# Unread products in the gaps of TensorE, later turns, panels awaited in parts, and a bias add moved behind a barrier

## The chip, the cores and the metric

The kernel runs on 1 core of one Trainium2 chip. The metric is the device time of one execution in microseconds (us). TensorE (PE) multiplies, VectorE (DVE) and ScalarE (ACT) work on tiles, GpSimd (POOL) fills, SyncE (SP) issues the transfers. TensorE's clock has two levels here, 2.4 GHz (shown as 1.00) and 1.2 GHz (shown as 0.50).

## The reference, cut to what matters

Four graph layers over 3125 nodes with 64 channels and 53125 edges sorted by dst, each followed by a residual sum and a layer norm:

```
x = layernorm(x + gcn2(x))              # h = x @ W; segment_sum(h[src], dst), twice, relu between
e = silu(silu([x[src], x[dst], d] @ eW1 + eb1) @ eW2 + eb2)
x = layernorm(x + silu([x, segment_sum(e, src)] @ nW1 + nb1) @ nW2 + nb2)
x = layernorm(x + relu(h_x + h_mu + relu(segment_sum(cat, src) @ W4.T)))     # message layer
x = layernorm(x + sum_k L^k x @ W[k] / k! + bias)    # polynomial of the graph Laplacian, k = 0..10
```

## The kernel before, in words

The nodes are cut into 25 blocks of 125 (B). The graph stands in SBUF as `t.mat`, a matrix of edge counts in bf16, 25 panels of 125 x 3128. A sum over edges for one block of nodes is 25 products of a 125x128 piece of `t.mat` with a 125x192 piece of `parts` (a float32 table split in three bf16 parts). Each layer is a block of its own, with a barrier of all engines behind it.

The layers in order of time: placing the edges and counting (to about 335 us), two GCN layers (`gcn_layers`, 335 to 459), the edge network (`edge_network`: a preparation block, 459 to 476, and a main block, 476 to 909), the message layer (`message_layer`, 909 to 1004), and the polynomial layer (`polynomial_layer`, 1004 to 1561).

`gcn_layers`: DVE reduces each sum (L1037), adds x, takes statistics (L1008, L1010), and scales finished rows chunk by chunk (`scale_rows`, L1021 to L1026); a chunk is scaled one sum after its last statistics.

`edge_network`, preparation: PE turns the node table (L1144) and multiplies it with eWb (L1154); ACT and DVE split the product in three parts (L1169, L1172, L1190, L1193). DVE adds the node bias nb2 to `t.xb` (L1180) ahead of that split. The edge rows of block 0 are being loaded meanwhile (`load_rows`, L1107 to L1110; `srow` and `drow`).

Main block: SP first loads rows of block 1 and panel 0 of `t.mat` back from DRAM. On DVE `rows_to_hot(0, 0)` (L1429, L1433) turns `srow` into one-hots, `dst_rows_to_hot(0, 0)` (L1437) does so with `drow`, and `split_p(0, 0)` (L1405 to L1411) splits the product that PE made in `product_p(0, 0)` (L1246) of the tile `xs[0]`, staged by ACT at L1334. Then come 25 blocks of 5 groups: `layer1` (L1258, L1264), silu, `layer2` (L1274), bias, silu, split, and `by_src` (L1287), the sum by source. After the last block the drain works off what is left: `layer2`, three `by_src`, `node1` (L1296, L1297), `node2` (L1302), while DVE centres the rows (L1511) and adds the last output (L1420), and ACT loads the table for the square root (L1392).

Panels 16 to 24 of `t.mat` hold temporaries of the edge network (`room`). SP loads panels 16 to 18 in the drain (L1240) and 19 to 24 in the message layer (L1579), two transfers each, all on the semaphore `tail_in`.

`message_layer`: PE turns the rows (L1692), multiplies them (L1708, L1726) in 7 groups; DVE splits the results into `parts` (L784 to L790). Then PE waits for all of `tail_in` and for all of `parts_ready`, and runs 25 sums (`spread`, L777) into two alternating banks. DVE takes each (L1851 to L1858), with statistics, and `centre` for each finished chunk, which waits for ACT's square root (`take_root`, L1637). ACT then scales (`set_x3`, L1645, L1649), PE turns the chunk (`turn_x3`, L1741), ACT keeps it (`keep_x3`, L1656), PE multiplies (`top_product`, L1753) and ACT keeps that (L1663). The chunks are blocks 0-3, 4-7, 8-11, 12-15, 16-19, 20-22, 23-24. `turn_x3(i)` stands behind sum 4i+7, `top_product(i)` behind the sum after it. ACT's order for each chunk is `take_root(i)`, `set_x3(i)`, `keep_y(i-1)`, `mask_y(i-1)`, `keep_x3(i)`. On DVE `centre(5)` stands ahead of the last reduction:

```
if b == NB - 1:
    take_stats(b - 1)
    centre(len(chunks) - 2)
dve.wait_ge(sums, b + 1)
```

`polynomial_layer`: 50 products (L1970), then 10 terms of 25 sums each (L1984). The first term waits for `last_kept`, a copy on DVE (L2028) that stands behind its bias add (L2014).

Of the kernel before, what the change touches and what calls it, by code (L numbers as in the profile page):

```python
# [12 lines left out]
P = 128  # L13
# [21 lines left out]
HEAD = 16  # L35
SPAN = 112
# [803 lines left out]
def gcn_layers(nc, a, c, t, l0, l1):  # L840

    with ExitStack() as s:
# [18 lines left out]
        chunks = [slice(lo, hi) for lo, hi in ((0, 8), (8, 16), (16, 23), (23, NB))]  # L861
# [187 lines left out]
def edge_network(nc, a, c, t, rows_d, m2_d, w, l2):  # L1049
# [14 lines left out]
    with ExitStack() as s:  # L1064
# [6 lines left out]
        o = NB * 3 * H  # L1071
        x1T = room[:, o:o + 2 * (NB + 1) * B].bitcast(F32)
        o += 2 * (NB + 1) * B
        srow = [room[:, o + i * DENSE:o + (i + 1) * DENSE] for i in range(2)]
# [4 lines left out]
        o += 2 * DENSE  # L1079
# [34 lines left out]
        tile_groups = [range(g, min(g + 4, NB)) for g in range(0, NB, 4)]  # L1114
        q_part = lambda g, r: q[0:B, tile_groups[g][0]:tile_groups[g][-1] + 1, r, :]
# [3 lines left out]
        with nc.Block() as block:  # L1119
# [19 lines left out]
            def _(pe):  # L1139
# [9 lines left out]
                for g, blocks in enumerate(tile_groups):  # L1149
                    pe.wait_ge(x1t_ready, g + 1)  # L1150
                    if g >= 2:
                        pe.wait_ge(q_cut, g - 1)
                    for i, b in enumerate(blocks):
                        last = nc.tensor.matmul(ps_z2[g % 2][0:B, i * H:(i + 1) * H], x1T[:, b * B:(b + 1) * B],  # L1154
                                                eWb[:], start=True, stop=True)
                    last.then_inc(q_ps, 1)

            @block.scalar
            def _(act):
                for g, blocks in enumerate(tile_groups):  # L1160
# [4 lines left out]
                                   ).then_inc(x1t_ready, 1)  # L1165
                for g in range(len(tile_groups) + 1):
# [8 lines left out]
            def _(dve):  # L1175
# [3 lines left out]
                dve.wait_ge(turned, len(tile_groups))  # L1179
                S(nc.vector.tensor_tensor(t.xb[:], t.xb[:], nb2[:].unsqueeze(1).broadcast_to([B, NB, D]), ALU.add))  # L1180
# [18 lines left out]
        (panels_in, rows_hot, staged, pre_done, e1_ready, z2_done, biased, silu2_done,  # L1199
         cut, mid_done, split_done, hot_ready, seg_done, agg_ready, n1_ready, z1_ready, out_ready, out_kept, stats, aggregated, xs_ready, p_ps, p_ready,  # L1200
         step) = map(sem, (
             "panels_in", "rows_hot", "codes_staged", "pre_done", "e1_ready", "z2_done", "biased", "silu2_done",
             "high_cut", "mid_done", "split_done", "onehots_ready", "seg_done", "agg_ready", "n1_ready", "z1_ready", "out_ready", "out_kept", "stats_taken", "aggregated",
             "xs_ready", "p_product", "p_ready", "net_step"))
# [9 lines left out]
        with nc.Block() as block:  # L1214
            @block.sync
            def _(sp):
# [21 lines left out]
                for i in range(HEAD, HEAD + 3):  # L1238
                    for to, of in spans(t.mat[:, i, :], m2_d[i]):
                        sp.dma_start(to, of).then_inc(l2.tail_in, 16)  # L1240

            @block.tensor
            def _(pe):
# [77 lines left out]
                product_p(0, 0)  # L1321
# [3 lines left out]
                by_src(z, 0, NG - 3)  # L1325
                by_src(z, 0, NG - 2)
                by_src(z, 0, NG - 1)
                node1(z, 0)
                node2(z, 0)

            @block.scalar
            def _(act):
# [51 lines left out]
                stage_x(0, 0)  # L1384
# [10 lines left out]
            def _(dve):  # L1395
# [29 lines left out]
                def rows_to_hot(b, k):  # L1425

                    if not first(b):
# [3 lines left out]
                        .broadcast_to([P, ST, DUP])).then_inc(staged, 1)  # L1431
                    dve.wait_ge(src_in[k], 8 * (b - k) + 16)
# [62 lines left out]
                rows_to_hot(0, 0)  # L1495
                dst_rows_to_hot(0, 0)
                split_p(0, 0)
# [21 lines left out]
def l2_weights(nc, ctx):  # L1519
# [6 lines left out]
    w.w_in, w.tail_in = (ctx.enter_context(nc.semaphore(n)) for n in ("L2_weights_in", "L2_tail_in"))  # L1526
# [11 lines left out]
def message_layer(nc, a, c, t, m2_d, l2):  # L1538


    with ExitStack() as s:
# [20 lines left out]
         kept, var, root, centred, x3_set, x3_scaled, x3_turned, x3t, w_top_in, w_top_set, x3_last, y_ps, y_kept, y_masked, deg_set, droot, deg_step, step) = map(sem, (  # L1562
# [3 lines left out]
             "x3_last_scaled", "y_product", "y_kept", "y_masked", "deg_set", "deg_root", "degrees_done", "msg_step"))  # L1566
# [5 lines left out]
        with nc.Block() as block:  # L1572
            @block.sync
            def _(sp):
                sp.wait_ge(feat_clear, 1)
                sp.dma_start(feat[D:D + 2, :], a["node_vec1"].partition_broadcast(2)).then_inc(nv_in, 16)
                for i in range(HEAD + 3, NB):
                    for to, of in spans(t.mat[:, i, :], m2_d[i]):
                        sp.dma_start(to, of).then_inc(l2.tail_in, 16)  # L1579
# [12 lines left out]
            def _(act):  # L1592
# [32 lines left out]
                act.wait_ge(deg_step, 1)  # L1625
# [60 lines left out]
            def _(pe):  # L1686
# [42 lines left out]
                pe.wait_ge(l2.tail_in, 32 * (NB - HEAD))  # L1729
                pe.wait_ge(parts_ready, len(groups))  # L1730

                def turn_x3(i):
# [3 lines left out]
                    else:  # L1736
                        pe.wait_ge(x3_last, 1)
# [31 lines left out]

            @block.vector  # L1770
            def _(dve):
# [47 lines left out]
                v.reciprocal(t.scale[:], t.root_deg[:]).then_inc(deg_step, 1)  # L1819
# [23 lines left out]
                for b in range(NB):  # L1843
# [17 lines left out]
                    if b >= 2 and b - 2 in ends[:-2]:  # L1861
# [11 lines left out]
                                ALU.mult).then_inc(x3_last, 1)  # L1873
# [738 lines left out]
```

## Time and profile before

| | |
|---|---|
| time, median of 3 runs | 1563.66 us (1562.77 to 1566.78) |
| time of the profiled execution | 1562.83 us |
| its span, first to last instruction | 1560.8 us |
| mean granted clock | 0.972 |
| PE busy | 1392.3 us, 89% of the span |
| DVE busy | 1207.8 us, 77% |
| ACT busy | 623.9 us, 40% |

Busy time is the sum of an engine's instructions. The granted clock is a mean, so a stretch at 0.75 is half its time at each level. In a row of the timeline, what stands in brackets is the idle time of the engine before the instruction and what ended it. PE rows are matmuls, PEld rows their weight loads, SPq rows the issue of transfers.

### The profile page before, as it was taken

The numbers are of one execution on the slowest core, as the hardware profiler recorded it, in microseconds if no ns is written. First come the engines' busy times: TensorE is split into PE (matmuls) and PEld (weight loads), VectorE is DVE, ScalarE is ACT, GpSimd is POOL, SyncE is SP. The second block draws the span as 40 slices with busy tenths as digits, with TensorE's granted clock in tenths as the row PEclk, the third lists the DMA queues.
The fourth block names the chain that finished last, engine by engine and source line by source line (L and its number), as shares of the span: only waits on it lengthen the run. The fifth ranks groups of instructions, "written<-read, shape, count | busy, mean of one in ns | idle before, by whom it ended". The sixth has DMA issues, their size and how long they took to land. (4 is left out here: it accounts for less than half of the span.)

```text
span 1560.8 us, 43036 instructions
## 1 busy us (share of the span) xinstructions
PE 1392.3 (89%) x16795; PEld 1286.9 (82%) x16795; DVE 1207.8 (77%) x3558; ACT 623.9 (40%) x1167; POOL 40.3 (3%) x81
## 2 busy tenths in 40 slices
PE   1845488889988999999999979899999999999997
PEld 1534466679986888888888849899999999999997
DVE  6899888855557888888888876677677677677676
ACT  0279799941116777777777742400000000000000
POOL 2111000000000000000000000000000000000000
PEclk9989799989999999999999979999999999999999
DMA  1000045430015454453232170000000000000000
GB/s 28 2 0 0 6 142 160 145 108 23 2 42 140 131 153 129 121 157 112 78 115 77 39 183 1 6 2 2 1 2 2 1 2 2 2 2 2 2 7 18
DMA packets 36900, 83.82 MB, mean 54 GB/s; under 512 B 22829, under 2 KB 23861, under 8 KB 36767
## 3 DMA queue, kind: packets, MB, share of 16 engines
q1 hardware_dynamic: 33633, 81.46, 18.4%
q8 instruction: 93, 1.52, 0.4%
q10 hardware_dynamic: 2880, 0.37, 0.2%
q14 instruction: 38, 0.31, 0.1%
q0 software_dynamic: 256, 0.15, 0.1%
HBM read 60.76 MB, written 21.14 MB: 52 GB/s over the span
## 5 line engine op out<-in xcount | busy, mean ns | idle before, releaser
L1984 PE MATMUL L_psA<-L_parts,mat 125*128 125x192 bf16 x3125 | 258.6, 246 | 0.4 <-issue 0.4
L1984 PE MATMUL L_psA<-second,mat 125*128 125x192 bf16 x3125 | 259.0, 246 | 0.0
L1984 PEld LDWEIGHTS L_psA<-L_parts,mat 125*128 125x128 bf16 x3125 | 257.9, 98 | 0.6 <-issue 0.6
L1984 PEld LDWEIGHTS L_psA<-second,mat 125*128 125x128 bf16 x3125 | 257.6, 98 | 0.6
L1264 PEld LDWEIGHTS L_ps_pre<-L_drow,mat 128*128 128x128 bf16 x2250 | 128.3, 98 | 30.0 <-issue 0.6
L1931 ACT COPY L_wk<-L_Wk 128x64 f32<-128x64 f32 x8 | 1.6, 242 | 378.1 <-PE L_psA L1984 378.1
L2040 DVE TENSOR_REDUCE L_sumr<-L_psA 125x64 f32<-125x192 f32 x225 | 80.4, 357 | 71.7 <-PE L_psA L1984 71.6
L1264 PE MATMUL L_ps_pre<-L_drow,mat 128*128 128x32 bf16 (+3 forms) x2250 | 132.7, 212 | 0.0
L684 PE MATMUL ps_count<-onehot 128*128 128x125 bf16 x1200 | 107.4, 219 | 15.2 <-DVE onehot L647 7.7
L1453 DVE TENSOR_TENSOR L_e<-L_e,mat 128x512 f32<-128x512 f32 x125 | 86.1, 689 | 40.4 <-ACT L_e L1351 40.4
L647 DVE TENSOR_TENSOR onehot<-iota_bf,codes 128x1024 bf16<-128x1024 bf16 x150 | 100.6, 686 | 18.0 <-PE ps_count L684 16.8
L886 PE MATMUL L_psA<-L_gparts,mat 125*128 125x192 bf16 x1250 | 111.2, 249 | 0.2 <-DVE L_sumr L993 0.2
L886 PEld LDWEIGHTS L_psA<-L_gparts,mat 125*128 125x128 bf16 x1250 | 106.6, 101 | 1.0 <-DVE L_sumr L993 0.4
L1287 PE MATMUL L_ps_agg<-L_hot,mat 128*128 128x125 bf16 x1500 | 103.5, 219 | 3.8 <-DVE mat L1458 3.8
L684 PEld LDWEIGHTS ps_count<-onehot 128*128 128x128 bf16 x1200 | 87.4, 98 | 23.2 <-DVE onehot L647 12.5
L1258 PE MATMUL L_ps_pre<-mat,L_pp 125*128 125x512 bf16 x375 | 102.4, 381 | 2.8 <-DVE L_pp L1411 2.8
L1445 DVE TENSOR_TENSOR L_e<-L_ps_z,L_eb 128x512 f32<-128x512 f32 x125 | 85.8, 686 | 21.4 <-PE L_ps_z L1274 19.8
L1287 PEld LDWEIGHTS L_ps_agg<-L_hot,mat 128*128 128x128 bf16 x1500 | 93.8, 98 | 5.6 <-DVE mat L1458 4.2
L1350 ACT ACTIVATE mat<-L_e 128x512 bf16<-128x512 f32 x125 | 78.9, 631 | 39.1 <-DVE L_e L1445 36.0
L1355 ACT CAST mat<-L_e 128x512 bf16<-128x512 f32 x125 | 77.0, 616 | 38.3 <-DVE L_e L1453 37.4
L1458 DVE TENSOR_TENSOR mat<-L_e,mat 128x512 bf16<-128x512 f32 x125 | 85.0, 680 | 0.3 <-ACT mat L1355 0.3
L426 PE MATMUL ps_slot<-rows,ohr 128*128 128x208 bf16 x450 | 45.9, 258 | 43.2 <-DVE rows L409 38.7
(329 smaller groups left out, 2387.3 us busy)
## 6 DMA issues: line engine op xcount, KB each, us to landing
L_drow<-rows_d SPq DMA_DIRECT2D x25, 728.0 KB
mat<-m_d SPq DMA_DIRECT2D x25, 684.2 KB
mat<-rows_d SPq DMA_DIRECT2D x25, 640.0 KB, 4.4
m_d<-panel SPq DMA_DIRECT2D x13, 684.2 KB
m_d<-xb SPq DMA_DIRECT2D x12, 684.2 KB
L_drow<-rows_d SPq DMA_DIRECT2D x25, 84.5 KB
mat<-m_d SPq DMA_DIRECT2D x25, 79.4 KB
m_d<-panel SPq DMA_DIRECT2D x13, 79.4 KB
```

What stands on the lines that cost most here:

```text
L647: nc.vector.tensor_tensor(to.rearrange("p e (m t) -> p e m t", t=DUP), c.iota1_bf[:].rearrange("p (m t) -> p m t", t=DUP).unsqueeze(1).bro ...
L684: last = nc.tensor.matmul(to, rows, cols[:, 0:B], start=True, stop=more is None)
L886: last = nc.tensor.matmul(acc(layer, b)[:, 0:3 * D], t.mat[0:B, kb, b * B:b * B + P], parts[layer][:, kb].rearrange("p r d -> p (r d)"), s ...
L1258: nc.tensor.matmul(ps_pre[bank][:, 0:hi - lo], pp[k][:, r, :], srow[k][0:B, lo:hi], start=(r == 0), stop=False)
L1264: last = nc.tensor.matmul(ps_pre[bank][:, to:to + n], w, drow[k][:, of:of + n], start=False, stop=(r == 2 and cc == pieces[-1][0]))
L1287: last = nc.tensor.matmul(ps_agg[k][:, 0:B], e2_parts[bank][:, part, i * H:(i + 1) * H], hot[bank][:, i, 0:B], start=(cc == 0 and part == ...
L1350: nc.scalar.activation(e2_parts[buf(k, g)][:, 0, :], e, ACT.Silu)
L1445: nc.vector.tensor_tensor(e2[buf(k, g)][:].rearrange("p (i h) -> p i h", h=H), ps_z2[bank][:].rearrange("p (i h) -> p i h", h=H), eb2[:].u ...
L1453: nc.vector.tensor_tensor(e, e, e2_parts[buf(k, g)][:, 0, :], ALU.subtract).then_inc(cut, 1)
L1458: nc.vector.tensor_tensor(part[:, 2, :], e2[buf(k, g)][:], part[:, 1, :], ALU.subtract).then_inc(split_done, 1)
L1984: last = nc.tensor.matmul(ps[:, 0:3 * D], t.mat[0:B, kb, b * B:b * B + P], parts[src][:, kb].rearrange("p r d -> p (r d)"), start=(kb == 0 ...
L2040: v.reduce_sum(r, ps[0:B, 0:3 * D].rearrange("p (r d) -> p d r", r=3), X).then_inc(bank_free, 1)
```

## The change

`hold_clock(nc, c, ps, n)` issues n matmuls of the bf16 identity with itself, 128 x 512, into a PSUM bank that nobody reads. It is called in nine places. Further:

- GCN: the last two row chunks are 16-21 and 22-24 (16-22 and 23-24 before).
- Edge network, preparation: the tile `xs[0]` is staged and multiplied there, and `srow[0]` is turned into one-hots in place of the add of nb2. The add follows in the main block, behind `stage_codes(0, 0)` (the first half of what was `rows_to_hot`), and `split_p(0, 0)` comes first.
- `room` is laid out anew, so that SP loads four panels in the drain (`FREED`) and five in the message layer. They count on three semaphores, panels 16-19, 20-21 and 22-24 (`LATE`).
- Message layer: the first sum waits piece by piece for the parts and the panels that it reads. `turn_x3(i)` stands behind sum 4i+8. `deg_step` and `x3_last` become one semaphore.

```diff
+FREED = 4
+LATE = (16, 20, 22)
+def hold_clock(nc, c, ps, n):
+    for _ in range(n):
+        nc.tensor.matmul(ps[:].rearrange("p (r n) -> p r n", n=P), c.ident_bf[:],
+                         c.ident_bf[:].unsqueeze(1).broadcast_to([P, 4, P]), start=True, stop=True)
...
-        chunks = [slice(lo, hi) for lo, hi in ((0, 8), (8, 16), (16, 23), (23, NB))]
+        chunks = [slice(lo, hi) for lo, hi in ((0, 8), (8, 16), (16, 22), (22, NB))]
...
+                pe.wait_ge(xs_ready, 1)
+                nc.tensor.matmul(ps_p[0:B, 0:H], xs[0][:], eWa[:], start=True, stop=True).then_inc(p_ps, 1)
+                hold_clock(nc, c, ps_pre[1], 11)
...
+                act.wait_ge(zeroed, 1)
+                act.wait_ge(x1t_ready, 1)
+                nc.scalar.copy(xs[0][:], x1T[:, 0:B]).then_inc(xs_ready, 1)
...
-                dve.wait_ge(turned, len(tile_groups))
-                S(nc.vector.tensor_tensor(t.xb[:], t.xb[:], nb2[:].unsqueeze(1).broadcast_to([B, NB, D]), ALU.add))
+                dve.wait_ge(src_in[0], 16)
+                S(nc.vector.tensor_scalar(srow[0][0:B, :], srow[0][0:B, :], c.row1[0:B, :], None, ALU.is_equal))
...
-                for i in range(HEAD, HEAD + 3):
+                for i in range(HEAD, HEAD + FREED):
                     for to, of in spans(t.mat[:, i, :], m2_d[i]):
-                        sp.dma_start(to, of).then_inc(l2.tail_in, 16)
+                        sp.dma_start(to, of).then_inc(l2.tail_in[late_panel(i)], 16)
...
-                product_p(0, 0)
+                hold_clock(nc, c, ps_pre[1], 9)
                 in_pairs(pe, NB, body)
                 z = NB - 1
                 layer2(z, 0, NG - 1)
                 by_src(z, 0, NG - 3)
+                hold_clock(nc, c, ps_pre[0], 8)
                 by_src(z, 0, NG - 2)
+                hold_clock(nc, c, ps_pre[0], 8)
                 by_src(z, 0, NG - 1)
                 node1(z, 0)
+                hold_clock(nc, c, ps_pre[0], 1)
                 node2(z, 0)
+                hold_clock(nc, c, ps_pre[0], 8)
...
-                rows_to_hot(0, 0)
+                split_p(0, 0)
                 dst_rows_to_hot(0, 0)
-                split_p(0, 0)
+                stage_codes(0, 0)
+                nc.vector.tensor_tensor(t.xb[:], t.xb[:], nb2[:].unsqueeze(1).broadcast_to([B, NB, D]), ALU.add
+                                        ).then_inc(nb_added, 1)
+                dve.wait_ge(nb_added, 1)
...
-                pe.wait_ge(l2.tail_in, 32 * (NB - HEAD))
-                pe.wait_ge(parts_ready, len(groups))
...
-                turned_after = {4 * i + 7: i for i in range(5)}
+                turned_after = {4 * i + 8: i for i in range(5)}
                 for b in range(NB):
                     if b >= 2:
                         pe.wait_ge(kept, b - 1)
-                    spread(pe, nc, t.mat, b, parts, psT[b % 2]).then_inc(sums, 1)
+                    for kb in range(NB):
+                        if b == 0:
+                            pe.wait_ge(parts_ready, kb // 4 + 1)
+                            if kb in LATE:
+                                pe.wait_ge(l2.tail_in[late_panel(kb)], 32 * sum(late_panel(i) == late_panel(kb)
+                                                                                for i in range(HEAD, NB)))
+                        last = nc.tensor.matmul(psT[b % 2][:, 0:3 * D], t.mat[0:B, kb, b * B:b * B + P],
+                                                parts[:, kb].rearrange("p r d -> p (r d)"), start=(kb == 0),
+                                                stop=(kb == NB - 1))
+                    last.then_inc(sums, 1)
                     if b in turned_after:
                         turn_x3(turned_after[b])
                     if b - 1 in turned_after:
                         top_product(turned_after[b - 1])
+                top_product(4)
                 for i in range(5, len(chunks)):
+                    hold_clock(nc, c, psG, 1)
                     turn_x3(i)
+                    hold_clock(nc, c, psG, 2)
                     top_product(i)
+                hold_clock(nc, c, psG, 3)
```

## Rows read from the trace of the kernel before

**Rows 1.** The page, part 2: granted TensorE clock, 40 slices of the span.
```profile
PEclk9989799989999999999999979999999999999999
```

**Rows 2.** The chain of waits that ended last: start, length, what.
```profile
1012.41 103.35 PE L_psA L1984 x1250
```

**Rows 3.** Windows of 10 us: length, busy time of each engine, clock, DMA.
```profile
510.00:520.00 10.00, 10.00 (x130) 8.89 (x129) 8.33 (x20) 7.49 (x14) 0.00 (x0) 1.00 0.74 210
...
960.00:970.00 10.00, 9.31 (x110) 9.07 (x108) 7.08 (x30) 3.86 (x15) 0.00 (x0) 1.00 0.01 2
```

**Rows 4.** Timeline, end of the two GCN layers: start, length, engine, line.
```profile
455.67 0.36 DVE L1037 TENSOR_REDUCE L_sumr<-L_psA 125x64 f32<-125x192 f32 x1 [1.09 <-PE L_psA L886]
...
456.56 0.59 DVE L1021 TENSOR_TENSOR xa<-xa,L_mean_var 125x448 f32<-125x448 f32 x1
...
457.84 0.22 DVE L1008 BATCH_NORM_STATS2 L_bn<-xa 125x6 f32<-125x64 f32 x1
```

**Rows 5.** Timeline, preparation block of the edge network.
```profile
464.44 1.82 DVE L1180 TENSOR_TENSOR xb<-xb,L_nb 125x1600 f32<-125x1600 f32 x1 [1.53 <-PE L_ps_pre L1144]
...
465.35 0.59 ACT L1169 CAST mat<-L_ps_z 125x512 bf16<-125x512 f32 x1 [0.58 <-PE L_ps_z L1154]
```

**Rows 6.** Timeline, opening of the edge network's loop.
```profile
476.43 0.88 DVE L1433 TENSOR_SCALAR mat<-mat,row 125x2560 bf16<-125x2560 bf16 x1
...
479.13 0.29 DVE L1411 TENSOR_TENSOR L_pp<-mat,L_pp 125x128 bf16<-125x128 f32 x1
...
479.57 1.44 PE L1258 MATMUL L_ps_pre<-mat,L_pp 125*128 125x512 bf16 x3 [2.22 <-DVE L_pp L1411]
...
484.18 1.14 PE L1274 MATMUL L_ps_z<-L_eW,L_e 128*128 128x128 f32 x8
...
494.96 0.82 PE L1258 MATMUL L_ps_pre<-mat,L_pp 125*128 125x512 bf16 x3 [0.54 <-DVE L_pp L1411]
```

**Rows 7.** Timeline, drain of the edge network.
```profile
901.95 0.84 PE L1287 MATMUL L_ps_agg<-L_hot,mat 128*128 128x125 bf16 x12 [1.96 <-DVE mat L1458]
...
904.64 1.44 PE L1287 MATMUL L_ps_agg<-L_hot,mat 128*128 128x125 bf16 x12 [1.84 <-DVE mat L1458]
...
906.22 1.76 DVE L1511 TENSOR_TENSOR xa<-xa,src 125x1536 f32<-125x1536 f32 x1
...
908.07 1.28 ACT L1392 ACT_TABLE_LOAD   x1
...
908.11 0.68 PE L1302 MATMUL L_ps_n<-L_nW,L_z 128*125 128x64 f32 x2 [0.46 <-ACT L_z L1366]
```

**Rows 8.** Timeline, opening of the message layer.
```profile
912.84 6.33 SPq L1579 DMA_DIRECT2D mat<-m_d  x12
...
914.51 1.93 PE L1708 MATMUL L_psM<-second,L_W3T 128*64 128x500 f32 x2
...
923.41 1.05 PE L1708 MATMUL L_psM<-L_x2T,L_W3T 128*64 128x500 f32 x2
```

**Rows 9.** Timeline, the first of the message layer's 25 sums.
```profile
934.91 0.23 DVE L790 TENSOR_TENSOR L_parts<-src,L_parts 125x64 bf16<-125x64 f32 x1
...
935.67 9.50 PE L777 MATMUL L_psT<-L_parts,mat 125*128 125x192 bf16 x93 [2.93 <-DMA mat<-m_d]
...
938.97 0.36 DVE L1851 TENSOR_REDUCE dense<-L_psT 125x64 f32<-125x192 f32 x1 [2.88 <-PE L_psT L777]
```

**Rows 10.** Timeline, one turn among the sums.
```profile
984.80 1.06 ACT L1649 ACTIVATE xa<-xb,scale 125x64 f32<-125x64 f32 x4
...
985.92 0.62 PE L1741 MATMUL L_psM<-ident,xa 125*64 125x125 f32 x4 [0.69 <-ACT xa L1649]
...
986.82 0.57 ACT L1656 COPY x3T<-L_psM 64x500 f32<-64x500 f32 x1
```

**Rows 11.** Timeline, last sum and end of the message layer.
```profile
999.04 0.36 DVE L1851 TENSOR_REDUCE dense<-L_psT 125x64 f32<-125x192 f32 x1 [0.56 <-PE L_psT L777]
...
1003.90 0.27 ACT L1663 COPY xa<-L_psZ 125x128 f32<-125x128 f32 x1 [0.74 <-PE L_psZ L1753]
```

**Rows 12.** Timeline, opening of the polynomial layer.
```profile
1011.96 0.35 DVE L2028 COPY src<-L_psA 125x64 f32<-125x64 f32 x2
...
1012.41 3.79 PE L1984 MATMUL L_psA<-L_parts,mat 125*128 125x192 bf16 x44 [0.39 <-issue]
```

More of the change, by code:

```diff
@@ L35, with late_panel @@
 HEAD = 16
+FREED = 4
+LATE = (16, 20, 22)
+def late_panel(i):
+    return sum(i >= first for first in LATE) - 1
 SPAN = 112
@@ L1071, in edge_network @@
         o = NB * 3 * H
+        srow = [room[:, o + i * DENSE:o + (i + 1) * DENSE] for i in range(2)]
+        o += 2 * DENSE
+        assert o >= FREED * MW
         x1T = room[:, o:o + 2 * (NB + 1) * B].bitcast(F32)
         o += 2 * (NB + 1) * B
-        srow = [room[:, o + i * DENSE:o + (i + 1) * DENSE] for i in range(2)]
         drow = [sb(f"drow{i}", [P, HOT], BF16) for i in range(2)]
@@ L1114, in edge_network @@
         tile_groups = [range(g, min(g + 4, NB)) for g in range(0, NB, 4)]
+        (panels_in, rows_hot, staged, pre_done, e1_ready, z2_done, biased, silu2_done,
+         cut, mid_done, split_done, hot_ready, seg_done, agg_ready, n1_ready, z1_ready, out_ready, out_kept, nb_added, stats, aggregated, xs_ready, p_ps, p_ready,
+         step) = map(sem, (
+             "panels_in", "rows_hot", "codes_staged", "pre_done", "e1_ready", "z2_done", "biased", "silu2_done",
+             "high_cut", "mid_done", "split_done", "onehots_ready", "seg_done", "agg_ready", "n1_ready", "z1_ready", "out_ready", "out_kept", "bias_added", "stats_taken", "aggregated",
+             "xs_ready", "p_product", "p_ready", "net_step"))
         q_part = lambda g, r: q[0:B, tile_groups[g][0]:tile_groups[g][-1] + 1, r, :]
@@ L1197, in _ @@
                                           ALU.mult, ALU.max))
[L1199 to L1204, printed above, removed]
         first = lambda b: isinstance(b, int) and b == 0
@@ L1383, in _ @@
                 act.sem_inc(agg_ready, 1)
-                stage_x(0, 0)
                 in_pairs(act, NB, body)
@@ L1423, in keep_out, with stage_codes @@
                                             ).then_inc(out_kept, 1)
-                def rows_to_hot(b, k):
+                def stage_codes(b, k):
                     if not first(b):
@@ L1431, in rows_to_hot @@
                         .broadcast_to([P, ST, DUP])).then_inc(staged, 1)
+                def rows_to_hot(b, k):
+                    stage_codes(b, k)
                     dve.wait_ge(src_in[k], 8 * (b - k) + 16)
@@ L1525, in l2_weights @@
     w.mix = sb("mix", [P, 2 * D], F32)
-    w.w_in, w.tail_in = (ctx.enter_context(nc.semaphore(n)) for n in ("L2_weights_in", "L2_tail_in"))
+    w.w_in = ctx.enter_context(nc.semaphore("L2_weights_in"))
+    w.tail_in = [ctx.enter_context(nc.semaphore(f"L2_tail{i}_in")) for i in range(3)]
     return w
@@ L1561, in message_layer @@
         (feat_clear, zeroed, nv_in, x2_root, x2_set, turned, x2t, hmu_ps, hmut, z_ps, parts_ready, nv_set, w_set, g_ps, g_set, sums,
-         kept, var, root, centred, x3_set, x3_scaled, x3_turned, x3t, w_top_in, w_top_set, x3_last, y_ps, y_kept, y_masked, deg_set, droot, deg_step, step) = map(sem, (
+         kept, var, root, centred, x3_set, x3_scaled, x3_turned, x3t, w_top_in, w_top_set, y_ps, y_kept, y_masked, deg_set, droot, degrees_and_last, step) = map(sem, (
              "feat_clear", "zeroed", "nv_in", "x2_root", "x2_set", "x2_turned", "x2T_ready", "hmu_product", "hmuT_ready", "z_product",
@@ L1576, in _ @@
                 sp.dma_start(feat[D:D + 2, :], a["node_vec1"].partition_broadcast(2)).then_inc(nv_in, 16)
-                for i in range(HEAD + 3, NB):
+                for i in range(HEAD + FREED, NB):
                     for to, of in spans(t.mat[:, i, :], m2_d[i]):
-                        sp.dma_start(to, of).then_inc(l2.tail_in, 16)
+                        sp.dma_start(to, of).then_inc(l2.tail_in[late_panel(i)], 16)
                 sp.wait_ge(hmu_ps, len(groups))
@@ L1736, in turn_x3 @@
                     else:
-                        pe.wait_ge(x3_last, 1)
+                        pe.wait_ge(degrees_and_last, 2)
                     if i >= 2:
```

9 lines of the change are left out of this document (4 added, 5 removed).

## The prediction

> **What bounds the kernel now.** I began with the row of the granted clock [rows 1]. It is not full in four places: slice 12 (450 to 480 us, with 13 beside it), slices 24 and 25 (900 to 940), and slice 26 (around 1005). Each is a border between two layers. Then the chain of waits [rows 2]: from 1012 us on it is nothing but TensorE's sums, 1250 products in 103.35 us, which is 2.07 us for a sum of 25, at full clock. The change touches nothing there, so that half of the span stays. Windows over the rest show PE busy without a gap inside the edge network's loop [rows 3]. There too a microsecond gained at the start is a microsecond gained at the end, and none can be gained inside. What remains are the borders, read in the timeline one by one: about 455 to 485, 897 to 942, and 999 to 1012. PE does little work in them, some of it at 1.2 GHz.
>
> **Price of an unread product.** Three products over 512 columns take 0.82 us at full clock and 1.44 at half [rows 6]. A single one is shown as 0.38, so a further one costs (0.82 - 0.38)/2 = 0.22 at full clock and about twice that, 0.43, at half. These are the same shape as `hold_clock`'s.
>
> **The change, part by part.** Gains have a minus.
>
> 1. GCN chunks. Today the last reduction (455.67) is followed by the scaling of seven blocks, and the last statistics start only at 457.84 [rows 4]. With six blocks in that chunk it is done one sum earlier, where DVE has 1.09 us idle. It takes some 1.2 us, so it runs over by 0.1. Saved: 457.84 - 456.56 = 1.28, less that 0.1, less 2 x 0.59/7 = 0.15 for one more block in the last chunk's two large operations: **-1.1** (0.8 to 1.3).
>
> 2. Preparation. The bias add (1.82 us) ends at 466.26; the cast for which DVE could start its first cut ends at 465.94 [rows 5]. The one-hots of `srow` take 0.88 [rows 6] and start when their rows have landed, before the cast is there as I read it. From there the split runs on DVE and ACT without slack, so: **-0.3** (bound 0, if the rows land a microsecond later). PE's added product and 11 unread ones, 0.4 + 11 x 0.22 = 2.8 us, lie under the last 3 us of that split, in which PE is idle. Without that cover the barrier would move.
>
> 3. Opening of the loop, order. `layer1` waits for the last DVE split, over at 479.42 [rows 6]. `srow` (0.88) and the codes (0.1) no longer stand ahead: **-0.9**. The add of nb2 lands behind, on a DVE that waits for `layer2` until 485, over four microseconds after it. It is hidden at 1.8 us. Queued behind it is the first bias add, for which PE waits later.
>
> 4. Opening, clock. From 479.57 to `layer2` at 484.18 are 4.6 us. The first three products alone take 1.44 where 0.82 is the price at full clock [rows 6]. At full clock the stretch is 3.2 to 3.4. **-1.3**, if the unread products keep the clock over the barrier. PE is idle for under a microsecond there, between the 11 and the 9. The 9 take 9 x 0.22 = 2.0 us and fit in the 2.4 us before `layer1` may start. If the clock is down anyway they take 3.9 and `layer1` starts 1.5 us late: bounds -1.6 and +1.5.
>
> 5. Drain. The second `by_src` at full clock takes 0.84, the third 1.44 at half; `node2` takes 0.68 [rows 7], and the two before it fall in the same clock. At full clock this path is 0.6 + 0.5 + 0.3 = 1.4 shorter. The 8 products (1.7 us) fit the waits of 1.96 and 1.84. But two others are late next. DVE's centring ends at 907.98 whatever PE does [rows 7], and 0.7 us of its work follow: 908.7 against 909.5 now. And the last 8 products start behind `node2`, at about 907.3, and end at 909.0. They, not ACT's table load (1.28, from about 906.9), release the barrier. So **-0.5** (-0.8 to 0).
>
> 6. Opening of the message layer, clock. `hidden(0)` takes 1.93 at 914.5 and 1.05 once the clock is up [rows 8]; PE's low clock sits on the path from the first turn to 919, some 3 us in all. But after the last unread product PE idles about 1.5 us, works for 1, idles again for 1.5 until DVE has the small weights. In the drain the clock fell between waits of 1.96 and 1.84 us with 0.8 of work between [rows 7]. I expect it to fall here as well, later than today, and rise sooner: **-1.2** (0 to -3.0).
>
> A rule of the Trainium skill bears on this ("TensorE: Matmul & The Clock Gate", What's actually happening): the monitor that gates the clock runs free, it doesn't start with the kernel. By that the opening would go one way in one execution and another in the next. The runs shown differ by 4 us; no row here says whether this is why.
>
> 7. First sum. Today PE waits until 935.67, for the transfers by the trace, with the last parts ready at 935.14, and the clock drops in that wait: the first reduction starts only at 938.97 [rows 9]. With waits of their own 24 of 25 products run ahead of the last parts, and the sum ends at 935.3: 3.6 us sooner. The second sum was still 0.7 us slow from the clock. DVE is not through with the degrees until 936.1, which holds the third sum by 0.3. **-4.0**. The panels must be there: twelve transfers for six panels, issued from 912.84 on [rows 8], landed by 935.6; that is 3.5 us or so a panel, so five end 3 us sooner, at 932, and panel 22 is asked for at about 934. If they came no sooner than now, only the clock and the overlap of the first 22 panels would be gained, 3.2. Together with 6 the slack of 2 us allows most of what the clock could give.
>
> 8. Later turns. At each turn PE waits 0.69 us for ACT's scaling [rows 10]. 2.06 us later ACT has it. DVE is busy for 7.1 us of ten here and PE for 9.3 [rows 3]; ten become 9.3 without the waits, and PE stays the bound: four turns, -2.8. The fifth is another matter. `turn_x3(4)` now stands behind sum 24 and ACT keeps it in 0.57 [rows 10], and only behind that in ACT's order comes the root for which `centre(5)` waits, ahead of DVE's last reduction. That reduction starts about 1.8 us after its sum is there, against at once [rows 11]. Today it comes 3.4 us after sum 23 (a turn with its wait stands between), then 3.9. Behind it ACT is busy with chunk 5 (2 x 0.8 for the scaling, then a kept y and a kept turn) when the last root is asked for, another 0.7. And three unread products stand behind the last product, 0.65 against 0.3 for ACT's copy. Lost: 0.5 + 0.7 + 0.3 = 1.5. Net **-1.3** (-2.5 to 0).
>
> 9. Polynomial. The products at half clock cost 1.6 us, but the first term waits for DVE's copy, over at 1012.31 [rows 12], behind its bias add. PE would be done earlier and wait: **0**. If its clock falls in that wait, the first sums run at half rate: up to +1.7.
>
> Sum: 1.1 + 0.3 + 0.9 + 1.3 + 0.5 + 1.2 + 4.0 + 1.3 = 10.6. From the profiled execution's 1562.8 that is 1552.2. The median of the runs shown is 0.8 above it, so **1553.0**.
>
> **The rivals.**
>
> A. The clock is held everywhere. Then part 6 gives 3.0 and part 5 its 0.8, the tail of the message layer goes without loss: 1553.0 - 1.8 - 0.3 - 1.2 = 1549.7. For it: the gaps left are all below 2 us. Against: two such gaps brought it down in the drain.
>
> B. The clock is not held over the barriers. The unread products run at 0.43 and stand in the way: part 4 turns from -1.3 to +1.5, part 5 to 0, part 6 to 0, part 9 adds up to 1: 1553.0 + 2.8 + 0.5 + 1.2 + 1.0 = 1558.5. For it: it is down at 479.57 after a wait of 2.22 us [rows 6]. Against: no gap that long is left at the loop's opening.
>
> C. The order and the waits do little: the sums stay bound by transfers and DVE, or the root's wait at the end eats the turns. Part 7 gives 1.7 (its clock alone), part 8 nothing: 1553.0 + 2.3 + 1.3 = 1556.6.
>
> D. Slower, by one mechanism: the new places of `srow` and `x1T` in `room` make the products of the edge loop slower. PE has no idle time there [rows 3], and there are 25 blocks. From 10.6/25 = 0.42 us a block on the gain is gone, from 0.6 it is a loss by over 0.3%; at 0.8 the time is 1553.0 + 20 = 1573. Nothing in the rows speaks for it but that PE has no slack.
>
> **How the numbers follow.** Forecast 0.50, A 0.16, B 0.13, C 0.18, D 0.03. 0.3% is 4.7 us, about what a measurement of this kernel can tell from no change: faster is below 1559.0. The forecast, A and C are faster, and most of B (its upper end reaches 1560 with a slow median). A remainder for parts that I took as independent and that aren't makes it 0.85 faster, 0.12 same, 0.03 slower. The range takes in A, C and the forecast with their bounds, and the middle of B: 1548.0 to 1558.5.
>
> **What would show it.** Right: clock 1.00 around 480 us and in the drain; `layer1` starting under 3 us after the barrier; the first reduction of the message layer 4 us or more sooner counted from that layer's start; no wait of PE for L1649 inside the sums; DVE waiting for ACT's root just ahead of its last reduction; the first polynomial term no sooner after the barrier than now. Wrong: a loop of the edge network longer than now between its first and last `layer1`; unread products of 0.43 in a row; the first sum waiting for panel 20 or 22.

## The result and the profile after

The changed kernel takes 1551.34 us (median of 4 runs, 1549.31 to 1553.36) against 1563.62 before; the ratio is 0.9918, with a 95% interval from 0.9897 to 0.9939. The forecast was 1553.0. The medians lie 12.3 us apart, the two profiled executions 10.0; runs of one kernel spread by 4 us. The profiled execution took 1552.80 us with a span of 1551.3, against 1562.83 and 1560.8.

The granted clock over the span (the page, part 2, answers to [rows 1]): the 24th slice, 897 to 936 us, reads 9 instead of 7. The fifth reads 8 instead of 7, and that one lies in code that the change doesn't touch. The line shows no more, for the other lost stretches are too short for a slice of 39 us. Line numbers below are those of the kernel that a row is of: `layer1` is L1281 in the changed kernel, `by_src` L1310, the unread products L794.

```profile
PEclk9989899989999999999999999999999999999999
```

I cut the span at the same instructions in both timelines. The stretches' lengths in us:

| from ... to | before | after | change | forecast |
|---|---|---|---|---|
| start ... last reduction of the GCN layers | 455.67 | 455.79 | +0.12 | 0 |
| ... end of the last scaling | 3.46 | 2.23 | -1.23 | -1.1 |
| ... first `layer1` product | 20.44 | 19.30 | -1.14 | -1.2 |
| ... first `layer2` product | 4.61 | 3.11 | -1.50 | -1.3 |
| ... last `layer1` (the loop) | 410.77 | 410.74 | -0.03 | 0 |
| ... first ACT instruction of the message layer | 14.89 | 14.49 | -0.40 | -0.5 |
| ... end of the last z product | 22.91 | 23.10 | +0.19 | -1.2 |
| ... third reduction of the sums | 11.04 | 7.13 | -3.91 | -4.0 |
| ... 24th reduction | 51.99 | 48.53 | -3.46 | -2.8 |
| ... first ACT instruction of the polynomial layer | 8.67 | 9.72 | +1.05 | +1.5 |
| ... first term | 7.96 | 7.97 | +0.01 | 0 |
| ... end of the span | 548.39 | 549.19 | +0.80 | 0 |

Up to the first term 10.30 us are gained. The first row is no effect of the change: the last four reductions are all 0.11 to 0.12 late, and the sums ahead of them are untouched. In the last row DVE's last instruction starts 540.89 us behind the first term in both (1553.30 and 1543.00); the 0.8 lies behind it, where the output is stored.

**GCN layers** (timeline, answers to [rows 4]). The scaling of six blocks stands ahead of the last reduction and doesn't hold it: it starts 0.28 us behind the start of the last product in both kernels. The last statistics follow at 456.67, not after another scaling.

```profile
455.79 0.36 DVE L1053 TENSOR_REDUCE L_sumr<-L_psA 125x64 f32<-125x192 f32 x1
...
456.67 0.19 DVE L1024 BATCH_NORM_STATS2 L_bn<-xa 125x6 f32<-125x64 f32 x1
```

**Preparation and opening of the loop** (timeline, [rows 5, 6]). `srow`'s rows have landed at 462.7, two microseconds before ACT's first cast is done, for which DVE now waits 1.23 us. Behind the barrier PE runs nine unread products of 0.22 us, and then `layer1`'s three take 0.82, where they took 1.44. The granted clock is 1.00 from 463 us on to the loop. The bias add of 1.82 us lies in DVE's wait for `layer2`.

```profile
462.73 0.89 DVE L1209 TENSOR_SCALAR mat<-mat,row 125x2560 bf16<-125x2560 bf16 x1 [0.93 <-DMA mat<-rows_d]
...
464.94 1.49 DVE L1219 TENSOR_TENSOR mat<-L_ps_z,mat 125x512 f32<-125x512 f32 x2 [1.23 <-ACT mat L1198]
...
475.25 2.10 PE L794 MATMUL L_ps_pre<-ident_bf 128*128 128x512 bf16 x9 [1.04 <-PEq L1142]
...
477.29 1.82 DVE L1528 TENSOR_TENSOR xb<-xb,L_nb 125x1600 f32<-125x1600 f32 x1
...
477.32 0.82 PE L1281 MATMUL L_ps_pre<-mat,L_pp 125*128 125x512 bf16 x3
...
480.43 1.14 PE L1297 MATMUL L_ps_z<-L_eW,L_e 128*128 128x128 f32 x8
```

**Drain** (timeline, [rows 7]). The third `by_src` takes 0.83 instead of 1.44. DVE's last work ends at 904.82 and ACT's, behind its table load, at 904.69, but the eight unread products end at 905.38. The message layer starts 0.3 us after them.

```profile
900.87 0.83 PE L1310 MATMUL L_ps_agg<-L_hot,mat 128*128 128x125 bf16 x12
...
903.49 1.89 PE L794 MATMUL L_ps_pre<-ident_bf 128*128 128x512 bf16 x8
...
904.49 0.20 ACT L1418 ACTIVATE src<-eps 1x1 f32<-1x1 f32 x1
...
904.64 0.18 DVE L1549 BATCH_NORM_AGGREGATE src<-src 125x2 f32<-125x6 f32 x1
...
905.66 0.32 ACT L1628 ACTIVATE src<-src,eps 125x25 f32<-125x25 f32 x1 [0.97 <-PEq L1237]
```

**Opening of the message layer** (windows of 1 us: length, PE busy, clock, DMA share, GB/s; then the timeline, [rows 8]). PE has nothing to do in most of 906 and all of 908 to 909, and the clock goes down at 909.3 (the mean of that microsecond is 0.66). `hidden(0)` (L1742) is at half rate as before.

```profile
906.00:907.00 1.00, 0.16 (x2) 1.00 0.40 123
...
908.00:909.00 1.00, 0.00 (x0) 1.00 0.00 0
...
909.00:910.00 1.00, 0.93 (x6) 0.66 0.76 113
...
910.13 1.93 PE L1742 MATMUL L_psM<-second,L_W3T 128*64 128x500 f32 x2
```

**First sum** (timeline, [rows 9]). Twenty-four products run right behind the last z product; the last one waits 0.47 us for its parts. No wait for a panel. DVE takes the first sum at 932.03, when it is through with the degrees, not when the sum is ready.

```profile
928.60 2.15 PE L1799 MATMUL L_psT<-L_parts,mat 125*128 125x192 bf16 x24
...
931.21 13.97 PE L1799 MATMUL L_psT<-L_parts,mat 125*128 125x192 bf16 x165 [0.47 <-DVE L_parts L806]
...
932.03 0.29 DVE L1896 TENSOR_REDUCE dense<-L_psT 125x64 f32<-125x192 f32 x1
```

**Turns and the end of the layer** (timeline, [rows 10, 11]). A turn has no idle time ahead of it. At the end ACT takes `keep_x3(4)` (986.84), then the root for chunk 5, DVE waits 0.78 us for it and reduces the last sum only then. The last root costs a second such wait, 0.82. From the 24th reduction (984.42) to the end of ACT's last copy it is 9.1 us; before it was 8.4.

```profile
957.63 0.59 PE L1773 MATMUL L_psM<-ident,xa 125*64 125x125 f32 x4
...
986.84 0.57 ACT L1690 COPY x3T<-L_psM 64x500 f32<-64x500 f32 x1 [1.64 <-PE L_psM L1773]
...
987.31 0.30 ACT L1671 ACTIVATE src<-src,eps 125x3 f32<-125x3 f32 x1
...
987.64 0.18 DVE L1885 RECIPROCAL src<-src 125x3 f32<-125x3 f32 x1 [0.78 <-ACT src L1671]
...
987.73 0.33 DVE L1896 TENSOR_REDUCE dense<-L_psT 125x64 f32<-125x192 f32 x1
...
990.85 0.17 DVE L1885 RECIPROCAL src<-src 125x2 f32<-125x2 f32 x1 [0.82 <-ACT src L1671]
...
993.26 0.27 ACT L1697 COPY xa<-L_psZ 125x128 f32<-125x128 f32 x1 [0.74 <-PE L_psZ L1785]
```

**Polynomial layer** (timeline, [rows 12]). PE is through with its products at 1000.0 and waits 2.07 us for DVE's copy, which ends at 1002.00, 7.86 us behind the layer's first ACT instruction (994.14). Before it was 7.86 too (1012.31 - 1004.45).

```profile
1001.65 0.35 DVE L2073 COPY src<-L_psA 125x64 f32<-125x64 f32 x2
...
1002.11 4.12 PE L2029 MATMUL L_psA<-L_parts,mat 125*128 125x192 bf16 x48 [2.07 <-issue]
```

### The profile page after: what moved, and what is told of

Read it like the earlier page. It is cut to its first block and busy times, and to the rows that moved or that the text cites. A ratio compares the mean times of both kernels' runs of the same rounds, so it can differ in the third digit from the quotient of the medians.

```text
span 1551.3 us, 43147 instructions
## 1 busy us (share of the span) xinstructions
PE 1395.7 (90%) x16849; PEld 1285.3 (83%) x16849; DVE 1208.8 (78%) x3558; ACT 625.3 (40%) x1167; POOL 40.1 (3%) x81
## 5 line engine op out<-in xcount | busy, mean ns | idle before, releaser
L1310 PE MATMUL L_ps_agg<-L_hot,mat 128*128 128x125 bf16 x1500 | 102.9, 218 | 0.4 <-DVE mat L1488 0.2
L1281 PE MATMUL L_ps_pre<-mat,L_pp 125*128 125x512 bf16 x375 | 101.6, 379 | 0.6 <-DVE L_pp L1437 0.6
L1310 PEld LDWEIGHTS L_ps_agg<-L_hot,mat 128*128 128x128 bf16 x1500 | 93.3, 98 | 2.8 <-DVE mat L1488 1.3
```

Source lines behind the costliest of these rows:

```text
L1281: nc.tensor.matmul(ps_pre[bank][:, 0:hi - lo], pp[k][:, r, :], srow[k][0:B, lo:hi], start=(r == 0), stop=False)
L1310: last = nc.tensor.matmul(ps_agg[k][:, 0:B], e2_parts[bank][:, part, i * H:(i + 1) * H], hot[bank][:, i, 0:B], start=(cc == 0 and part == ...
```

## The experiments

Eleven kernels ran. "Changed" is the changed kernel; stretches are those of the table. Where the clock is the same, an untouched stretch repeats to 0.04 us from kernel to kernel, so the profiles tell more than the times, which spread by 1 to 6 us: no single one of experiments 5 to 8 differs from the changed kernel in time beyond the intervals. Every kernel computes all of the reference.

**1. No products.** `hold_clock` issues nothing.

```diff
-    for _ in range(n):
+    for _ in range(0):
```

> The changed kernel without any unread product. Theory (order and waits do most; the products give the loop's opening and little else): the clock is down when layer1 starts, so the stretch from the first layer1 product to the first layer2 is about 4.6 us instead of 3.1 (+1.5); the drain is at half clock again, but its barrier no longer waits for the last 8 products, +0.4; the message layer's opening is as slow as with them, 0; the end of the message layer 0 to +0.5. Time 1553 to 1554, about 2 us over the changed kernel. Rival (the products do most of the work): 1557 to 1560.

Measured: 1555.24 us (median of 5, 1553.31 to 1559.32; ratio to before 0.9947, 0.9929 to 0.9965). `layer1` is at half rate again:

```profile
477.02 1.46 PE L1281 MATMUL L_ps_pre<-mat,L_pp 125*128 125x512 bf16 x3 [5.48 <-DVE L_drow L1467]
...
481.59 1.14 PE L1297 MATMUL L_ps_z<-L_eW,L_e 128*128 128x128 f32 x8
```

The stretch is 4.57 us: of the gain of 1.50 us 1.46 is gone. From the loop's end to the message layer it is 14.89, as before the change (14.49 changed). The message layer's opening is 22.87, no longer than the changed kernel's 23.10, but 1.4 longer than the 21.48 of experiment 10. From the last reduction to the polynomial layer it is 6.86 against 6.41: the barrier is 0.33 shorter without the three products (0.28 against 0.61), but the clock is low from 992 on. From the last GCN reduction to the first term the products are worth 2.0 us of the 10.4 in this profile (548.35 - 546.32); the order and the waits are the rest. The stretches of parts 1 to 3 keep their gain without the products (2.23 and 19.27).

**2. Products alone.** The kernel before with the nine groups, and nothing else of the change (`hold_clock(nc, c, ps_pre[1], 9)` stands behind `product_p(0, 0)`).

> The kernel before with the nine groups of unread products and nothing else. Theory: only the loop's opening and the drain gain, 1.5 + 0.4 us, so about 1561.5. Rival (products do most): 1554 to 1557. With product_p(0, 0) still behind the barrier the clock could also fall in the opening, then about 1563.

Measured: 1560.3 us (median of 11; ratio 0.9981, 0.9970 to 0.9993). From the first `layer1` to `layer2` it is 3.09 us (-1.52), the drain is 0.41 shorter, the barrier at the end of the layer 0.33 longer. Its opening of the message layer took 21.91, 1.0 less than before; the clock then fell in PE's wait for the panels (932 to 936 us), and the stretch to the third reduction took 11.78 instead of 11.04, so 0.7 of that went again. The gains of parts 4 and 5 need nothing but the products, and those of parts 1 to 3 don't come from them: their stretches stay at 3.46 and 20.44.

**3. All awaited.** The first sum waits for every panel and part.

```diff
-                        if b == 0:
-                            pe.wait_ge(parts_ready, kb // 4 + 1)
+                        if b == 0 and kb == 0:
+                            for i in range(3):
+                                pe.wait_ge(l2.tail_in[i], 32 * (4, 2, 3)[i])
+                            pe.wait_ge(parts_ready, len(groups))
+                        if False:
                             if kb in LATE:
```

> The changed kernel, but the first sum of the message layer waits for all panels and all parts, as before. Theory: the first sum starts with the last parts (2.6 us after the 24 products could start), 2.0 us are lost on it, and where the clock falls in that wait another 1.7 on the first two sums: +2 to +3.9 against the changed kernel, 1553.3 to 1555.2. Rival (the panels in the drain did it, five instead of six behind the barrier): under 1 us lost.

Measured: 1557.21 us (median of 5; ratio 0.9956, 0.9940 to 0.9972). From the last z product to the third reduction 10.64 us instead of 7.13: 3.5 lost, with the clock down from 930 to 934. In this profile the clock fell twice more, at the layer's end and at the first term, so its time says more than this stretch. PE waits for the parts:

```profile
929.66 8.58 PE L1802 MATMUL L_psT<-L_parts,mat 125*128 125x192 bf16 x82 [2.53 <-DVE L_parts L806]
```

**4. Turns early.** `turned_after = {4 * i + 7: i for i in range(5)}`.

> The changed kernel with turn_x3(i) behind sum 4i+7 again. Theory: each of the first four turns costs 0.88 us again (a period of 10.41 us for four sums in place of 9.53), +3.5; the last reduction no longer waits for ACT's root behind keep_x3(4), -1.0; together +2.4, about 1553.7. Rival (DVE limits the sums, the turns' waits were cover): no change, 1551.3.

Measured: 1557.19 us (median of 5; ratio 0.9945, 0.9927 to 0.9963). From the third to the 24th reduction 51.99 us, to the hundredth what it was before, with four waits of PE for ACT's scaling; from there to the next layer it is 9.01 instead of 9.72. That is a loss of 3.46 - 0.71 = 2.75 us against 2.4 expected.

```profile
958.07 0.62 PE L1773 MATMUL L_psM<-ident,xa 125*64 125x125 f32 x4 [0.69 <-ACT xa L1683]
...
968.48 0.62 PE L1773 MATMUL L_psM<-ident,xa 125*64 125x125 f32 x4 [0.70 <-ACT xa L1683]
```

**5. The fifth turn back.** `turned_after = {8: 0, 12: 1, 16: 2, 20: 3, 23: 4}`, and no `top_product(4)` behind the loop.

> The changed kernel with the fifth turn alone back behind sum 23 (turns behind 8, 12, 16, 20 and 23). Theory: the late fifth turn delays ACT's root and with it DVE's last reduction; now the reduction follows its sum at once and the stretch from the last reduction to ACT's last copy falls from 5.8 to about 5.1 us; the turn's 0.45 on PE moves ahead of sum 24. From the reduction of sum 23 to the end of the layer 8.4 instead of 9.1 us, so -0.7 in all. Rival (the end is bound by ACT's order of work, wherever the turn stands): no change or +0.5.

Measured: 1550.0 us (median of 4, 1548.81 to 1552.43; ratio 0.9912, 0.9889 to 0.9935). The last reduction comes 2.64 us behind the one before, instead of 3.31: -0.67, as forecast in sum. But from there to ACT's last copy it is 5.77 us, not 5.1. The second wait for a root, behind `set_x3(5)` and `keep_x3(5)` in ACT's order, is still there:

```profile
986.48 0.30 ACT L1671 ACTIVATE src<-src,eps 125x2 f32<-125x2 f32 x1
...
986.80 0.17 DVE L1884 RECIPROCAL src<-src 125x2 f32<-125x2 f32 x1 [0.81 <-ACT src L1671]
```

But this wait isn't a loss against the kernel before. From the 24th reduction to the end of ACT's last copy it is 8.41 us here, 8.39 before and in experiment 4, and 9.10 in the changed kernel: the last reduction comes 0.62 sooner than before, and ACT scales chunk 5 no sooner (2.75 us behind the 24th reduction here, 2.73 before, 3.43 in the changed kernel). So the whole 0.7 at the end comes from the late fifth turn.

**6. Opening filled.**

```diff
+                hold_clock(nc, c, psM[1], 5)
                 turn(0)
                 turn(1)
+                hold_clock(nc, c, psM[1], 6)
                 pe.wait_ge(w_set, 1)
```

> The changed kernel with 5 more unread products ahead of the first turn of the message layer and 6 behind its second. Theory: the clock falls in that opening because of the two gaps that the change leaves open; filled, it stays at full level, z(0) is 5.8 to 6.2 us behind the layer's first ACT instruction instead of 9.2, and 2.5 to 3.3 us are gained in every execution: median about 1548.5. Rival (small products with long latencies hold the path, not the clock): under 1 us gained. Rival 2: the parts' transfers become the bound, PE waits for panel 20 or 22 in the first sum and half the gain is lost.

Measured: 1549.52 us (median of 4, 1548.89 to 1550.09; ratio 0.9905, 0.9885 to 0.9925). From the layer's first ACT instruction to the last z product it is 19.96 us instead of 23.10. `hidden(0)` at full rate:

```profile
905.32 1.46 PE L794 MATMUL L_psM<-ident_bf 128*128 128x512 bf16 x6
...
907.41 1.05 PE L1744 MATMUL L_psM<-second,L_W3T 128*64 128x500 f32 x2
```

Against the 22.91 of before that is -2.95, the -3.0 of part 6's lower bound; against the profiles of the changed kernel in which the opening took 21.5 (experiments 3, 5, 8, 10) it is -1.5. The transfers kept up: the first sum waits 0.46 us for its last parts and for no panel. Elsewhere the clock was not held: it fell at 997.0, behind PE's wait for the first polynomial term, and the first reduction of that term came 3.78 us behind its first product instead of 2.26.

**7. Four behind.** `hold_clock(nc, c, ps_pre[0], 4)` behind `node2`.

> The changed kernel with 4 instead of 8 unread products behind node2. Theory: these products end last before the barrier (0.56 us after DVE, 0.69 after ACT); with 4 they end with DVE and ACT, and the message layer starts 0.5 us sooner relative to the loop's end. The clock falls earlier or as before. Rival (the barrier waits for DVE's centring): no change at the barrier.

Measured: 1554.01 us (median of 4, 1552.77 to 1555.03; ratio 0.9933, 0.9911 to 0.9951). The barrier comes 0.55 us sooner:

```profile
904.61 1.03 PE L794 MATMUL L_ps_pre<-ident_bf 128*128 128x512 bf16 x4
...
905.76 0.18 DVE L1549 BATCH_NORM_AGGREGATE src<-src 125x2 f32<-125x6 f32 x1
...
906.23 0.32 ACT L1628 ACTIVATE src<-src,eps 125x25 f32<-125x25 f32 x1 [0.42 <-PEq L1237]
```

DVE's last row ends at 905.94 and the next layer starts 0.29 later, so DVE is last now. The opening behind it takes 23.55 us, the longest of all profiles (the clock is low from 910 to 917), so in this execution the gain at the barrier is given back. Whether the missing products brought that isn't shown.

**8. Bias later.** The bias add of the polynomial layer stands behind the copy that the first term awaits.

```diff
-                S(v.tensor_tensor(t.xb[:], t.xb[:], bias[:].unsqueeze(1).broadcast_to([B, NB, D]), ALU.add))
                 start = S.n
...
                     less(0, src)
+                    if it == 0 and src == 0:
+                        v.tensor_tensor(t.xb[:], t.xb[:], bias[:].unsqueeze(1).broadcast_to([B, NB, D]), ALU.add
+                                        ).then_inc(late_masked, 1)
...
                 def last_term(it, src):
+                    dve.wait_ge(late_masked, 2)
```

> The changed kernel with the 1.8 us bias add of the polynomial layer behind the copy for which the first term waits. Theory: the first term waits for DVE, not for PE's products; PE's wait of 2.07 us at the term's start falls to under 0.4 and the time by 1.6 to 1.7. Rival (the term waits for the parts or for the products): no change. This is the counterpart to part 9 of the prediction: if it holds, a full clock in the products is worth something only with it.

Measured: 1551.03 us (median of 4, 1545.51 to 1551.87; ratio 0.9902, 0.9874 to 0.9930). The first term comes 6.22 us behind the layer's first ACT instruction instead of 7.97: -1.75, and PE waits 0.32. The median doesn't show it; in the profile the clock fell at the message layer's end (989 to 993), and the stretch ahead of this one took 1.1 longer.

```profile
1000.53 0.35 DVE L2072 COPY src<-L_psA 125x64 f32<-125x64 f32 x2
...
1000.98 3.21 PE L2029 MATMUL L_psA<-L_parts,mat 125*128 125x192 bf16 x37 [0.32 <-issue]
```

**9. All better.** Experiments 5 to 8 in one kernel.

> The changed kernel with the fifth turn behind sum 23, the message layer's opening filled, 4 products behind node2 and the later bias add of the polynomial layer. Steps measured one by one add to 0.55 + 3.0 + 0.65 + 1.75 = 6.0 us against the changed kernel's profiled execution, 5.0 against its median (its opening is sometimes the fast one): 1546.3. Rival (they compete: four products behind node2 leave a gap in which the clock falls anyway, and a filled opening only moves the wait to the transfers): 1548 to 1549.

Measured: 1547.45 us (median of 4, 1545.18 to 1548.59; ratio 0.9899, 0.9882 to 0.9915). Steps against the changed kernel: barrier -0.55, opening -3.13, end of the layer -0.69, first term -1.75, 6.1 in all. The four gains add up. The 3.13 counts from the first profile of the changed kernel; from that of experiment 10 it is 1.5. With the openings filled the clock is up from 463 us to the first term and beyond. The median is 3.9 us below the changed kernel's first one and 5.7 below that of the next experiment, which is the changed kernel measured on the same chip; the runs of either don't overlap with these.

**10. Unchanged**, the changed kernel once more.

> The changed kernel once more, to see how one program varies. Theory: its steps between the borders repeat to 0.1 us except where the clock's fall lands elsewhere: the message layer's opening takes 23.1 us from the layer's first ACT instruction to the last z product when the clock is low for 6.8 us in it, and 21.5 when it is low for 3.4; and the untouched layers ahead of the last GCN sum spread over 3 us. Times from 1549 to 1554. Rival (the spread comes from transfers or elsewhere): steps differ where the clock does not.

Measured: 1553.19 us (median of 4, 1551.89 to 1554.69; ratio 0.9930, 0.9914 to 0.9947). Its opening of the message layer takes 21.48 us, with the clock low for 3.4 us; the first profile's took 23.10, with 6.8. Its end of the layer, last reduction to last copy, takes 6.93 against 5.80, with the clock low from 989 to 992. The clock also falls at the end of PE's wait for the first term (1002.3), so that most of the first sum runs at half rate:

```profile
1003.00:1004.00 1.00, 1.00 (x8) 0.50 0.08 16
...
1002.31 5.86 PE L2029 MATMUL L_psA<-L_parts,mat 125*128 125x192 bf16 x49 [2.07 <-issue]
...
1006.22 0.36 DVE L2085 TENSOR_REDUCE L_sumr<-L_psA 125x64 f32<-125x192 f32 x1 [3.69 <-PE L_psA L2029]
```

The first reduction of the term comes 3.91 us behind its first product, where the first profile of the changed kernel has 2.26 (1004.37 - 1002.11). That is 1.65, the loss that part 9 named as up to 1.7. Nine of the profiles have this wait of 2.06 us with the products run at full clock ahead of it; in four (experiments 3, 4, 6, 10) the clock fell there, for 1.5 to 1.65.

**11. Three panels.** `FREED = 3`.

> The changed kernel, with three panels loaded in the drain and six behind the barrier, as before (the other waits as changed). Theory: the last panel lands about 3 us later than in the changed kernel, where some 3 us lie between the end of its traffic at 925 and the first sum's need at 930.5 less 2 us to landing; so PE waits 1 to 2.5 us in the first sum for panel 22, and the third sum comes up to 1.5 us later. Rival (the waits one by one did it all, the fourth panel nothing): no change.

Measured: 1552.82 us (median of 4, 1552.36 to 1557.58; ratio 0.9941, 0.9920 to 0.9962). PE waits 0.20 us ahead of panel 22, and the last product waits for its parts as before; the third reduction comes 7.12 us behind the last z product, as in the changed kernel (7.13).

```profile
930.33 4.92 PE L1799 MATMUL L_psT<-L_parts,mat 125*128 125x192 bf16 x52 [0.20 <-DMA mat<-m_d]
```

I had expected 1 to 2.5 us. The rival was right: the fourth panel in the drain is worth nothing here. (With an opening 3 us faster it would be needed sooner; that was not tried.)

## Why the prediction was right

The sum, 10.6 us, met 10.3 to the first term, and most parts hold by themselves. That it came so close is in part luck: part 6 missed by 1.4 in this profile and part 8 by 1.1 the other way.

- What bounds the kernel: the row of the clock doesn't show what I read from it. Slices 12, 13, 25 and 26 read 9; only slice 24 reads 7, and the other lower digits (slices 3, 5 and 9) lie in layers that the change leaves alone. The low clock at the borders is in the lengths of the timeline's rows.
- Parts 1 to 3 (GCN chunks, preparation, order): -2.3 forecast, -2.37 measured. Part 1's own terms add to 1.0, not 1.1. The last statistics came the 1.28 sooner; the overrun of 0.1 did not occur, and the third block in the last chunk cost 0.06, not 0.15.
- Part 4: right, and caused by the products (experiments 1 and 2).
- Part 5: right in what is late next. The eight products do release the barrier, and with four it is DVE (experiment 7).
- Part 6: mis-sized, and the size depends on the execution. The clock falls here in both profiles of the changed kernel, as I expected of it, for 6.8 us in one (+0.2) and for 3.4 in the other (-1.4). Counted from the layer's first ACT instruction it rises at 10.5 us in the first and at 7.2 in the other, where it was 9.9 before, so "sooner" held for one of the two. Over the eight profiles with the changed order and an opening left as it is, the stretch is 21.5 in four and 23.1 to 23.6 in four, 0.5 below the 22.91 of before on average. Filled, it gives the bound of 3 (experiment 6).
- Part 7: -4.0 against -3.91, and waiting for everything gives nearly all of it back (experiment 3: 3.5). I took an early fourth panel for a condition of it; with three, PE waits 0.20 us for panel 22 and nothing is lost (experiment 11). The rate was misread too: six panels from 912.84 to 935.6 are 3.8 us a panel, not 3.5.
- Part 8: mis-sized. The row's 0.69 us counts from the modelled end of PE's last product (0.25 us behind its start, where the next one starts after 0.08). By starts, the turn's first product comes 0.94 us behind the sum's last one before and 0.08 in the changed kernel. The period of four sums fell from 10.41 to 9.53, which is 0.88 a turn, 3.5 for four. The loss at the end was 1.05, not 1.5: the last reduction comes 3.31 us behind the one before, where it was 3.26 with the turn and its wait in between (3.4 by my reading); ACT's last copy comes 0.67 later behind it; the barrier costs 0.33 more. With the fifth turn back behind sum 23 (experiment 5) the 0.7 is gone and the barrier's 0.33 stays. The parts were sized -2.8 and +1.5, and came out at -3.46 and +1.05: -2.4 instead of -1.3.
- Part 9: right, both the zero (experiment 8 shows the copy as the bound) and the possible loss, which came in four of nine profiles (experiment 10).

Rival A, the clock held everywhere, came true in experiment 9 alone; with only the opening filled (experiment 6) it fell at the first term. Rival B did not occur: in every profile of a kernel with the products the clock was full over the loop's opening. C fell with experiments 3 and 4, which give back 3.5 and 2.7 us. D: the loop has the same length to 0.03 us. (The 0.6 us a block that I called a loss of over 0.3% comes to 25 x 0.6 - 10.6 = 4.4 us, just under 4.7.)

The rule of the Trainium skill ("TensorE: Matmul & The Clock Gate", What's actually happening) that the monitor which gates the clock isn't started by the kernel agrees with what the runs show. One program, profiled twice, has its clock low at 909.3 to 916.1 in one and at 910.2 to 913.6, 988.7 to 992.1 and 1002.3 to 1005.8 in the other. No run here shows what sets the places.

## What to carry to other kernels

Price a border between two layers by asking which engine's work ends last, then what is late next: here a faster PE gave nothing in the drain beyond DVE's centring and its own fill, and nothing in the polynomial's products. Unread products pay where the path goes through PE just behind the gap (1.5 us at the loop's opening; 1.5 to 3.1 in the message layer, by the execution, when both gaps were filled), cost up to their own length where they stand last before a barrier (0.55 us for four in the drain, 0.33 for three at the layer's end), and give nothing where another engine is the bound. Before a step is moved later in a loop, look at the order of each engine at the loop's end: what stood behind the step comes later too (0.7 us here).

## What the runs showed of the hardware

The untouched layers ahead of the last GCN reduction took 453.4 to 456.9 us in the thirteen profiled executions, with the same work. The two windows that follow (columns as above) are of experiments 6 and 7, whose code is the same up to there. From 342 to 348 us the one has a full clock and 71 products, the other 0.58 and 41:

```profile
342.00:348.00 6.00, 6.00 (x71) 1.00 0.20 49
```
```profile
342.00:348.00 6.00, 6.00 (x41) 0.58 0.13 35
```

So code that nobody touched spreads by 3.5 us, and a change worth 1 us can be read only in its own stretch. That the clock makes the whole spread isn't shown: its low stretches ahead of that reduction add to 44 to 51 us, and the execution with the least of them (experiment 4) is among the longest.

The clock also fell where PE was never idle for as much as 2 us: in the drain of the kernel before at 902.6, 0.7 us behind the end of a wait of 1.96 us [rows 7], and in the changed kernel at 909.3, 0.2 us behind gaps of 1.46 and 1.19 us with a microsecond of small products between. A gap of 2.06 us ahead of the polynomial's first term went without a fall in five profiles of nine.
